# Attention block: ScalarE issues the transfers of the shift, in place of SyncE

## What is computed

```python
xn = _layernorm(x, axis=-1)                                  # x: (32, 256, 128)
# attention
q = einsum('bsd,hde->bhse', xn, wq) + bq                     # k, v alike; h = 16, e = 8
scores = softmax(einsum('bhse,bhte->bhst', q, k) * scale)
att = einsum('bhst,bhte->bhse', scores, v)                   # -> (b, s, 128)
attn = att @ wo.T + bo
# feed-forward with a mix of each token and the one before it
xr = mu_r * xn + (1 - mu_r) * x_prev;  xk = mu_k * xn + (1 - mu_k) * x_prev
ffn = sigmoid(xr @ W_r.T) * (square(relu(xk @ W_k.T)) @ W_v.T)
out = x + attn + ffn
```

## Time and profile before

| | us |
|---|---|
| median of 3 runs | 506.4 (506.03 to 507.11) |
| the profiled execution | 506.4 |
| its span on the core | 504.6 |
| one steady batch (243.00 to 257.25) | 14.25 |

### The profile page before, as it was taken

One profiled execution on the slowest core, in us unless ns is written; L12 is line 12 of the kernel. 1 busy time (PEld: TensorE's weight loads), 2 busy tenths in 40 slices (PEclk: granted clock), 3 DMA queues, 4 the chain that ended last, 5 costly groups with the idle time before them and its releaser, 6 DMA issues.

```text
span 504.6 us, 15503 instructions
## 1 busy us (share of the span) xinstructions
PE 454.6 (90%) x5184; PEld 259.1 (51%) x5184; DVE 422.8 (84%) x882; ACT 389.2 (77%) x833; POOL 342.6 (68%) x615
## 2 busy tenths in 40 slices
PE   1388999899999999999999999999999999999995
PEld 1134555555555555555555555555555555555552
DVE  4297899889898999899998999989998999988831
ACT  1107888788888888888888888888888888888883
POOL 6656777677786777777876777678776777776220
PEclk9999999999999999999999999999999999999998
DMA  2442455344544443345444444454444434544200
GB/s 83 125 137 78 126 139 144 109 114 126 149 132 134 136 126 112 110 137 147 126 137 136 126 117 115 127 147 131 133 137 124 122 112 127 147 132 114 76 16 21
DMA packets 85837, 60.43 MB, mean 120 GB/s; under 512 B 6192, under 2 KB 73392, under 8 KB 85808
## 3 DMA queue, kind: packets, MB, share of 16 engines
q1 hardware_dynamic: 85808, 60.06, 42.2%
HBM read 29.89 MB, written 29.36 MB: 117 GB/s over the span
## 4 chain that ended last, share of the span: by engine, by line
PE 47%; DMA 14%; SPq 10%; issue 10%; POOL 8%; DVE 8%; ACT 2%; DVEq 0%; ACTq 0%; POOLq 0%
PE bank_exp L567 13%; PE bank_val L535 13%; DMA ops<-shift 12%; DVE neg_max L473 6%; SPq L236 5%; SPq L221 5%; PE bank_max L572 4%; PE misc_b L638 4%; POOL act_sq L327 4%; POOL qk_m L329 3%; PE misc_c L658 3%; PE misc_a L646 3%; PE misc_b L662 2%; PE misc_a L668 2%; ACT probs L399 1%
## 5 line engine op out<-in xcount | busy, mean ns | idle before, releaser
L473 DVE TENSOR_REDUCE neg_max<-bank_max 128x2 f32<-128x512 f32 x512 | 330.0, 687 | 47.4 <-PE bank_max L572 43.7
L399 ACT ACTIVATE probs<-bank_exp 128x512 f32<-128x512 f32 x512 | 279.3, 596 | 57.9 <-PE bank_exp L567 57.6
L567 PE MATMUL bank_exp<-ops 51*128 51x256 bf16 x1024 | 165.8, 271 | 22.6 <-DMA ops<-shift 17.8
L572 PE MATMUL bank_max<-ops 48*128 48x256 bf16 x1024 | 170.8, 278 | 10.6 <-DMA ops<-spill 8.1
L535 PE MATMUL bank_val<-probs,val 128*25 128x256 f32 x2048 | 136.3, 384 | 1.2 <-ACT probs L399 1.2
L567 PEld LDWEIGHTS bank_exp<-ops 51*128 51x128 bf16 x1024 | 66.1, 94 | 111.0 <-issue 60.7
L535 PEld LDWEIGHTS bank_val<-probs,val 128*25 128x25 f32 x2048 | 50.4, 103 | 51.8 <-issue 26.8
L572 PEld LDWEIGHTS bank_max<-ops 48*128 48x128 bf16 x1024 | 62.2, 95 | 18.3 <-DMA ops<-spill 8.5
L361 POOL TENSOR_TENSOR rstd<-var_eps,minus_half 128x2 f32<-128x2 f32 x32 | 22.9, 714 | 48.0 <-DVE var_eps L503 45.4
L317 POOL TENSOR_SCALAR xn<-x_in,moments,rstd 128x128 f32<-128x128 f32 x64 | 50.7, 798 | 0.1
L356 POOL TENSOR_TENSOR mixed_x<-mixed_x,xn_t 128x512 f32<-128x512 f32 x32 | 40.8, 1275 | 2.5
(11 more groups left out here) (59 smaller groups left out, 596.6 us busy)
## 6 DMA issues: line engine op xcount, KB each, us to landing
ops<-spill SPq DMA_DIRECT2D x128, 192.0 KB, 3.4
spill<-qk_h SPq DMA_DIRECT2D x64, 192.0 KB, 3.4
spill<-qk_m SPq DMA_DIRECT2D x64, 128.0 KB, 1.9
x_in<-x SPq DMA_DIRECT2D x32, 128.0 KB, 2.2
spill<-qk_l SPq DMA_DIRECT2D x32, 128.0 KB, 1.9
y_out<-y SPq DMA_DIRECT2D x32, 128.0 KB, 1.9
ops<-shift SPq DMA_DIRECT2D x128, 6.0 KB
w<-weights SPq DMA_DIRECT2D x1, 448.0 KB, 3.1
```

Of the source, the lines that this page charges most:

```text
L399: nc.scalar.activation(probs[g % 2][:, u % G, :, :], bank_exp[u % 2][:, :, :], ACT.Exp, scale=SCALE).then_inc(exp_done[u], 1)
L473: nc.vector.tensor_reduce(out=neg_max[hf][:, :, r, pr], in_=bank_max[v % 2][:, :, :], axis=AX_X, op=ALU.max, negate=True).then_inc(max_don ...
L567: exp_mm = nc.tensor.matmul(bank_exp[r][:, i, :], ops[p][rows, hf, 1, pr, i * P:(i + 1) * P], ops[p][rows, hf, 0, pr, :], start=True, stop ...
L572: max_mm = nc.tensor.matmul(bank_max[r][:, i, :], of[rows, max_hf, 0, max_pr, i * P:(i + 1) * P], of[rows, max_hf, 1, max_pr, :], start=Tr ...
```

## The change

`load_shift` and its two calls leave SyncE's program. `move_shift` in ScalarE's program takes the parity p of the `ops` buffer, and behind its copy it now waits for the copy's own semaphore and issues the two transfers. Sources, destinations, sizes and semaphores stay as they are, and so does the place of the copy.

```diff
-            def load_shift(half, p, count, before):
-
-                after(sp, shift_done[half], count)
-                after(sp, shift_in[half], before)
-                for r in range(2):
-                    sp.dma_start(ops[p][RG * r + KS:RG * r + KE, half, 0],
-                                 shift[half][3 * PR * r:3 * PR * (r + 1), :]).then_inc(shift_in[half], 16)
-
...
-                if live(0):
-                    load_shift(1, p, n(0), moved(-1, 2))
...
-                if live(1):
-                    load_shift(0, 1 - p, n(1), moved(0, 2))
...
-            def move_shift(half, count, before):
+            def move_shift(half, p, count, before):
                 act.wait_ge(shift_psum[half], count)
                 after(act, shift_in[half], before)
                 nc.scalar.copy(shift[half][:, :], shift_bank).then_inc(shift_done[half], 1)
+                act.wait_ge(shift_done[half], count)
+                for r in range(2):
+                    nc.scalar.dma_start(ops[p][RG * r + KS:RG * r + KE, half, 0],
+                                        shift[half][3 * PR * r:3 * PR * (r + 1), :]).then_inc(shift_in[half], 16)
...
-                        move_shift(1, n(0), moved(-1, 2))
+                        move_shift(1, p, n(0), moved(-1, 2))
...
-                        move_shift(0, n(1), moved(0, 2))
+                        move_shift(0, 1 - p, n(1), moved(0, 2))
```

## The result

The changed kernel takes 563.6 us (median of 5, 562.8 to 566.1) for 506.7 us before (median of 5, 506.0 to 508.6). The ratio is 1.112, with an interval of 1.109 to 1.115: slower. The profiled execution has a span of 564.3 us. A few executions of a kernel are slower than its others, and times and ratios leave them out: one of the new order on SyncE (552.4 us, at a granted clock of 0.77) and two of the three issues per half (669.8 and 670.7 us).

What follows compares the result with a forecast made beforehand. TensorE was taken as the bound by rate, with ScalarE's issues delaying its exponentials: 24 x 0.81 + 8 x 0.50 + 31 x 1.23 = 61.5 us on the 504.6 us span, plus 1.8 outside it: 568 us, range 525 to 597.

Steps and rivals of the forecast that it cites:

- TensorE's clock: TensorE's clock in steady batches: granted at 1.00 and over 80% busy, so it was ruled out as an alternative.
- The hold d: Time a pair of issues holds ScalarE's queue: 1.50 us for half 1, 1.48 for half 0, from SyncE's pairs.
- Half 1: Gate and exponentials 4 and 5 wait behind the issues; unit 8 starts 0.81 us later, 0.50 in 8 of 32 batches.
- Half 0: Exponentials 10 and 11 wait behind the issues; the values' matmuls come 1.23 us later, counted 31 times.
- A: ScalarE's queue: the issue doesn't hold ScalarE, or hardly, so only the gain is left: 489 us; chance 0.12.
- B: ScalarE's issues: cheap, 0.42 us each as for the large transfers: 527 us; chance 0.15.
- behind it nothing gives it back: Behind the values' matmuls of half 0: the 1.23 us delay stays, exponential 12 ending before unit 14 wants it.
- The formula: Delay per batch from the hold d: d - 0.69 us at half 1, d - 0.25 us at half 0.
- Rival C: ScalarE's issue of half 1 during SyncE's qk_m pair: one must wait, 596 or 582 us; chance 0.17 with other longer-issue reasons.
- Rival D: Engines run ahead enough that only ScalarE's rate counts, 15.12 us a batch: 533 us; chance 0.04.
- The gain: TensorE's wait for the shift of half 1 before L567, 0.55 us a batch: at most 17.8 us won in all.

Runs made afterwards that it cites:

- new order on SyncE: Against the kernel before, SyncE issues the shift of half 1 ahead of the two spills of qk_m; nothing moves to ScalarE: 503.8 us, ratio 0.994.
- three issues per half: The changed kernel with a third issue behind each pair on ScalarE, to an unused tile: 663.8 us, ratio 1.308.
- half 1 alone: Against the kernel before, ScalarE issues the shift pair of half 1 only, SyncE keeps that of half 0: 528.9 us, ratio 1.042.
- With one: Against the kernel before, ScalarE issues one of the two shift transfers of each half, SyncE the other: 514.7 us, ratio 1.014.
- half 0 alone: Against the kernel before, ScalarE issues the shift pair of half 0 only, SyncE keeps that of half 1: 544.3 us, ratio 1.074.
- four issues at half 1: ScalarE issues the pair of half 1 and two more transfers to an unread tile; half 0 stays with SyncE: 628.2 us, ratio 1.238.

## Why the prediction was right, point by point

The forecast of 568 us is 4 us above the measured 563.6, and the growth of 61.5 us was 56.9. The mechanism was right: ScalarE stands for the length of the issues, and TensorE waits for its exponentials in both halves. That the number came so near is in part luck. Three terms were too large, by 24 x 0.11, 8 x 0.14 and 31 x 0.10 us (the bullets below), 6.9 us in all, and TensorE's clock, put at nothing, gave up to 3 us of that back. By its steps:

- *The hold d.* 1.50 and 1.48 us were taken from SyncE's pairs; ScalarE's are 1.50 and 1.49. An issue takes 0.729 us (median) for 0.714. It was the likeliest case, and the rivals A (no hold) and B (0.42 us) are out. The Trainium skill says (Perfetto Trace Analysis, DMA Instruction, HWDGE) that the sequencer is free only once the issue is done; ScalarE's 1.57 us ahead of L391 agree. The sentence of the Trainium skill that spreading issues over engines only saves the time to issue, usually a small one (DMA: Bandwidth & Descriptors, Issuing engines are not separate DMA queues) holds here only where the issuing engine has room behind the issue: the same issues cost 1.13 us a batch at one place and none at the other.
- *Half 1.* +0.81 us foreseen, 0.70 measured. The way to unit 6 was right (1.18 foreseen, 1.17 measured); from unit 6 to unit 8 it takes 1.89 us, not 2.00. Where the loop turns, 0.50 was taken, and it is 0.36 (14.59 before, 14.95 with half 1 alone).
- *Half 0.* +1.23 foreseen; +1.01 up to unit 12 and 0.27 behind it, so 1.28 measured at the place, but 1.13 over the batch. So the size at the place was 0.05 us too small, and "behind it nothing gives it back" was wrong by 0.15 us, 4 us in all. Unit 15 started 0.36 us behind unit 14 before, because VectorE's maxima of units 12 and 13 ended just ahead of it; with TensorE later, VectorE is done in time and it is 0.24. Row one is of the kernel before (ending 254.86, unit 15 at 255.01), row two of after (ending 266.82, units 14 and 15 at 266.87 and 267.11):

```profile
253.57 1.29 DVE L473 TENSOR_REDUCE neg_max<-bank_max 128x2 f32<-128x512 f32 x2
```

```profile
265.53 1.29 DVE L465 TENSOR_REDUCE neg_max<-bank_max 128x2 f32<-128x512 f32 x2 [1.04 <-PE bank_max L564]
```

- *The formula.* With one and with three issues, d - 0.69 and d - 0.25, less those 0.14, give 0.38 and 3.3 us a batch (d of 0.73 and 2.20); at full clock it was 0.30 and 3.36.
- *Rival C, two engines issuing at once.* It did not happen: a pair of half 1 takes 1.49 us as one of half 0, beside a pair of SyncE at the same time. Of ScalarE's 128 issues 61 fall into one of SyncE's, and their median is 0.731 us for 0.729 of the others; SyncE's issue of qk_m takes 0.41 us with or without (timeline of SyncE after, ScalarE's pair being at 272.42):

```profile
272.39 0.88 SPq L228 DMA_DIRECT2D spill<-qk_m  x2
```

- *Rival D*, only ScalarE's total work counts, is refuted by the batch of 16.08 us where it had 15.12, and by half 0 alone: there ScalarE has 12.08 + 1.5 = 13.6 us of work, less than the 14.25, and the batch still grew by 1.13. Room counts where it is, not in sum.
- *TensorE's clock "is no rival"* was the wrong sentence. It cost this execution some 3 us (two batches of 31), and with one more issue per half some 50 us. That TensorE stays busy for over 80% of the time was no reason: with four issues at half 1 it is busy for 14.05 of the 16.46 us of a batch at full clock, and the clock fell in 27 of 31.
- *The gain.* "At most that wait" was right as a bound, but as an amount to be had it isn't: taken alone, it gives 3 us of 17.8, and 9 with one of the two waits behind it reduced. In the sum it did no harm, because there the wait was only replaced by a longer one.

## What to carry to other kernels

An issue is work of the engine that issues it, though no share of busy time shows it. Its price is the time by which it exceeds the room that is left before another engine waits for that one: 0.73 us were free behind exponential 13 and cost up to their full length behind the shift copy, where TensorE waits for the very next exponential. Before a wait is removed, look for what becomes ready just behind it. In the kernel before, in the batch of the rows, the loads for unit 14 landed 0.30 us ahead of it (254.35 for 254.65), and VectorE's maxima ended at 249.55 for unit 9 at 250.03, which by the lag of 0.15 us leaves 0.33 us of room (an estimate from these rows). Either is less than the 0.55 us of the wait, so not all of it could be had alone.

## What the runs showed of the hardware

- An issue of this small transfer (12 rows of `shift` into 3 rows of `ops`, 6 KB) takes 0.71 us on SyncE and 0.73 on ScalarE, more than the 0.42 of the loads of `ops`, thirty times its size. Why is left open.
- Issues of ScalarE and SyncE that ran at the same time did not lengthen each other here: 0.731 us for 0.729 (61 and 67 issues of the changed kernel).
- An instruction ahead of an issue in ScalarE's program may still run during it (the copy of val, 253.51 to 253.89, in an issue of 253.45 to 254.18); those behind it don't start.
- TensorE's clock fell to 0.50 behind stalls of 2.36 to 2.92 us (26 batches with four issues at half 1), and behind ones of 1.40 to 2.08 us in a few batches of other kernels (1.40 and 1.44 in the changed one). It did not fall behind the usual ones of 0.94 and 1.11 us, nor in other batches behind stalls of 1.40, 1.57, 1.86, 2.15 and 2.31 us. With three issues per half and two stalls a batch, 22 of 31 batches lost it (stalls of 1.4 to 1.9 us) and 8 kept it (1.7 to 1.9 us). What exactly decides is left open.
